# Writes of the attention outputs to DRAM issued by ScalarE instead of SyncE

## The reference, cut to what matters

```python
h = modulate(ln(x))
q, k, v = split(h @ W_qkv)            # 16 heads of 16
a = softmax(q @ k.T * 0.25 + mask)    # L0, L1, L3: all 1024 keys; L2: windows of 128
x = x + gate * ((a @ v) @ W_o)
h = modulate(ln(x))
a = softmax(q(h) @ k(ctx).T * 0.25)   # 77 keys; L2 keeps the 16 largest scores
x = x + gate * ((a @ v(ctx)) @ W_co)
x = x + gate * mlp(modulate(ln(x)))
```

## Time and profile before

| | |
|---|---|
| median of 3 runs | 3085.87 us (3081.41 to 3093.61) |
| profiled execution, device time | 3097.3 us |
| its span, first to last instruction | 3095.5 us |
| TensorE busy | 2704.0 us (87%) |
| VectorE busy | 2005.2 us (65%) |
| ScalarE busy | 1401.0 us (45%) |
| GpSimd busy | 644.9 us (21%) |
| DMA, mean busy share of 16 engines | 30% |
| mean granted TensorE clock | 0.907 |

### The profile page before, as it was taken

The page is one execution under the profiler, slowest core; times in us unless marked ns, Lnnn a source line. Parts: engine busy times, 40 slices in busy tenths (PEclk is TensorE's granted clock), DMA queues, the critical chain, the costliest instruction groups (busy, mean ns, idle before and its releaser), DMA issues.

```text
span 3095.5 us, 44651 instructions
## 1 busy us (share of the span) xinstructions
PE 2704.0 (87%) x13376; PEld 1240.5 (40%) x13376; DVE 2005.2 (65%) x4844; ACT 1401.0 (45%) x2569; POOL 644.9 (21%) x968
## 2 busy tenths in 40 slices
PE   6999999998799998989978767686679999999899
PEld 4433333335322533324454444554424342332456
DVE  6678488441668366765455568666896858886631
ACT  3255555661446464664534223322223736667341
POOL 1010011301221010131124134524312110112320
PEclk9799999899779998999988876797779999999799
DMA  6222214311532122332065424431121223122521
GB/s 211 63 63 63 79 36 135 117 31 59 176 92 62 59 78 87 103 106 65 28 187 173 112 78 149 136 93 37 64 89 32 60 51 109 53 63 88 158 84 36
DMA packets 254276, 275.90 MB, mean 89 GB/s; under 512 B 60485, under 2 KB 195423, under 8 KB 253663
## 3 DMA queue, kind: packets, MB, share of 16 engines
q1 hardware_dynamic: 242783, 271.58, 29.6%
q0 software_dynamic: 11264, 1.46, 0.3%
HBM read 157.36 MB, written 114.09 MB: 88 GB/s over the span
## 4 chain that ended last, share of the span: by engine, by line
PE 67%; DVE 16%; DMA 7%; issue 5%; POOL 2%; ACT 2%; SPq 2%; DVEq 0%; ACTq 0%; POOLq 0%
PE ring_a L1238 11%; PE ring_c L1312 10%; PE ring_b L1282 10%; PE ring_b L1335 7%; PE ring_a L1347 7%; PE ring_b L1281 4%; PE ring_a L1324 4%; PE ring_b L1196 3%; DVE row_max L1582 3%; DMA q_ring<-neg_max_parts 2%; PE ring_a L1335 1%; PE ring_b L1306 1%; DMA q_ring<-scr_q 1%; DVE bn_stats L1490 1%; PE ring_b L1270 1%
## 5 line engine op out<-in xcount | busy, mean ns | idle before, releaser
L1417 ACT ACTIVATE probs<-ring_b 128x512 f32<-128x512 f32 (+1 forms) x1728 | 906.3, 604 | 561.7 <-PE ring_b L1282 486.2
L1582 DVE TENSOR_REDUCE row_max<-ring_a 128x1 f32<-128x1024 f32 x512 | 602.8, 1219 | 133.9 <-PE ring_a L1238 130.6
L1282 PE MATMUL ring_b<-q_ring,k_ring 100*128 100x512 bf16 x1536 | 522.0, 389 | 24.0 <-DMA q_ring<-neg_max_parts 9.9
L1238 PE MATMUL ring_a<-k_ring,q_ring 96*128 96x512 bf16 x1536 | 481.7, 406 | 43.1 <-DVE row_max L1582 27.5
L1312 PE MATMUL ring_c<-probs,v_and_ones 128*17 128x512 f32 x3072 | 404.2, 605 | 3.6 <-ACT probs L1417 3.5
L1579 DVE CUSTOM_DVE_ANT_0 w_mlp<-ring_a,w_mlp 128x1024 bf16<-128x1024 f32 x256 | 302.8, 1222 | 72.9 <-PE ring_a L1238 71.0
L1693 POOL CAST neg_max_parts<-neg_max 16x128 bf16<-16x128 f32 x112 | 32.2, 287 | 1506.3 <-ACT neg_max L1411 1251.1
L1626 DVE TENSOR_TENSOR x_tok<-x_tok,ring_a 128x512 f32<-128x512 f32 x96 | 65.8, 687 | 364.1 <-PE ring_a L1347 210.3
L1238 PEld LDWEIGHTS ring_a<-k_ring,q_ring 96*128 96x128 bf16 x1536 | 129.7, 100 | 379.9 <-issue 302.8
L1282 PEld LDWEIGHTS ring_b<-q_ring,k_ring 100*128 100x128 bf16 x1536 | 146.3, 99 | 305.8 <-issue 198.0
L1335 PE MATMUL ring_b<-h_feat,w_mlp 128*128 128x512 f32 x512 | 236.3, 611 | 2.1 <-ACT h_feat L1391 1.7
(11 more groups left out here) (140 smaller groups left out, 3218.6 us busy)
## 6 DMA issues: line engine op xcount, KB each, us to landing
q_ring<-scr_q SPq DMA_DIRECT2D x128, 384.0 KB, 4.0
scr_q<-split SPq DMA_DIRECT2D x64, 384.0 KB, 3.1
k_ring<-scr_k SPq DMA_DIRECT2D x64, 384.0 KB, 4.9
scr_q<-split SPq DMA_DIRECT2D x64, 256.0 KB, 3.2
scr_out<-out_stage SPq DMA_DIRECT2D x128, 128.0 KB, 2.5
scr_out<-out_stage SPq DMA_DIRECT2D x64, 256.0 KB, 2.3
h_feat<-scr_out SPq DMA_DIRECT2D x56, 256.0 KB
reciprocals<-scr_recip SPq DMA_DIRECT2D x56, 256.0 KB
```

The source lines that it names most:

```text
L1238: last = mm(ps[:, half * BLOCK:(half + 1) * BLOCK], q[0:PARTS, h, t * P:(t + 1) * P], k_view(g)[0:PARTS, h, half * BLOCK:(half + 1) * BLOC ...
L1282: last = mm(ps[:, :], k_view(g)[0:ROWS, h, s.kt * P:(s.kt + 1) * P], q[0:ROWS, h, q0:q0 + BLOCK], start=not g.masked, stop=True)
L1417: f(PT[0:n, s.pt, :], ps[0:n, :], ACT.Exp, **kw).then_inc(b_evac, 1)
L1582: v.tensor_reduce(NM[:, s.nm, s.u:s.u + 1], ps, AX.X, ALU.max).then_inc(a_evac, 1)
```

## The change

The branch `put` moves from SP's program to ScalarE's. The list of steps, the condition and the DMAs stay as they are. On ScalarE's list a put now stands where the plan has it: after the copy into `out_stage` and often after one to three further ScalarE instructions of other steps.

```diff
         @block.sync
-                elif s.kind == "put":
-                    g, pv = s.g, s.of
-                    if "bn" in pv:
-                        sp.wait_ge(b_evac, pv.bn + 1)
-                    else:
-                        sp.wait_ge(c_evac, pv.c_n + 1)
-                    h0 = g.heads[0]
-                    n = len(g.heads) * VROWS
-                    for k, blk in enumerate(g.blks):
-                        sp.dma_start(O_SCR[g.b, h0:h0 + len(g.heads), :, blk * BLOCK:(blk + 1) * BLOCK].rearrange("h r t -> (h r) t"),
-                                     OST[k * n:(k + 1) * n, s.ost, :]).then_inc(ost_out[s.ost], 16)
         @block.scalar
+                elif s.kind == "put":
+                    g, pv = s.g, s.of
+                    if "bn" in pv:
+                        act.wait_ge(b_evac, pv.bn + 1)
+                    else:
+                        act.wait_ge(c_evac, pv.c_n + 1)
+                    h0 = g.heads[0]
+                    n = len(g.heads) * VROWS
+                    for k, blk in enumerate(g.blks):
+                        act.dma_start(O_SCR[g.b, h0:h0 + len(g.heads), :, blk * BLOCK:(blk + 1) * BLOCK].rearrange("h r t -> (h r) t"),
+                                     OST[k * n:(k + 1) * n, s.ost, :]).then_inc(ost_out[s.ost], 16)
```

## The result

The kernel after took 3114.18 us (median of 4 runs, 3108.43 to 3121.13) beside 3089.24 us of the kernel before in the same comparison (4 runs): ratio 1.0085, 95% interval 1.0054 to 1.0115, or +26 us. The change makes the kernel 0.7 to 0.9% slower. The forecast had the sign, and at +8 us too small a size, by a factor of about 3. 3114 lies in the stated range, and it is the number of the rival "full price", but that rival's mechanism is not what happened. The forecast's own band, 3083 to 3102, does not hold it: that the stated range does is owed to the room left for a rival which was wrong, and is luck.

The account below looks back on a forecast made before the run. TensorE, busy 87% of the span, was taken to bound the kernel. Terms 10 + 2 + 0 + 0 - 1 - 3 gave +8 us: 3105.3 us for the profiled execution, 3094 us carried to the median, range 3075 to 3118.

Parts of the forecast that it names:

- full price: Rival: on ScalarE the issue begins only when the exponential before it has ended; +28 us, 3114 us, chance 0.22.
- The forecast's own band: The span of the main case, a short stall of ScalarE: 3083 to 3102 around 3094 us, chance 0.48.
- SyncE gains nothing: On SP's queue, losing 192 issues (96 us) and the waits before them was counted as nothing.
- The landings give 3 us: Two put landings on the chain, 6.45 and 5.21 us, would shorten: 3 us gained, bounds 0 and 6.9.
- The last rival: Faster: SP's query loads no longer share its queue with puts, so their landings shorten; -17 us, 3069 us, chance 0.10.
- ScalarE prepares ahead, but not past an exponential that waits: On ScalarE, a put's issue can run beside an exponential that has begun, but not pass one still waiting.
- the cheap rival: Issues cost ScalarE under 0.5 us for two, or pass a waiting exponential, starting at the copy's end; 3083 us, chance 0.20.
- The forecast of 0.66 us late: At one full self-attention put, a pair's issue of 1.14 us makes ScalarE's next exponential 0.66 us late.
- The size of the loss: Full self-attention, 48 puts: TensorE loses 0.3 us on average at 33, 0 at the other 15; 10 us.
- The term for window and cross puts: Six back-to-back window puts at 0.3 us give 2 us; the 64 cross-attention puts 0, at most 2.
- the 1 us given back: A small part of TensorE's loss falls in front of a wait that exists anyway: minus 1 us.
- Later puts and what follows: Puts go out up to 1.5 us later, with `dense` and reciprocals following: 0, at most 5 us.

Follow-up runs that it names:

- e6: The kernel after, with SyncE still waiting for each copy where it issued the put but issuing nothing: +18 us over the kernel before.
- e9: The kernel after, unchanged, measured a second time: ratio 1.0066, +20 us over the kernel before.
- e10: e6 measured again, the kernel after with SyncE's old waits left in: ratio 1.0066, +20 us over the kernel before.
- e1: Against the kernel before, only the 48 full self-attention puts moved to ScalarE, window and cross-attention puts on SyncE: +21 us.
- e3: The kernel after, but ScalarE issues only the first DMA of each pair and SyncE the second: 0 us over the kernel before.
- e7: The kernel after, but each pair's second DMA issued two exponentials later or before another kind of step: +3 us over the kernel before.

## Why the prediction was right and wrong

*SyncE gains nothing: right.* e6, e9 and e10 show it from both sides.

*The landings give 3 us: not borne out.* The two landings of the earlier trace rows did get shorter, by 3.6 us together, but four are on the chain now, 14.3 us in sum where it was 11.7 (pieces of the chain after):

```profile
1357.98 4.25 DMA scr_out<-out_stage
...
1664.74 3.85 DMA scr_out<-out_stage
...
1965.92 4.26 DMA scr_out<-out_stage
...
1992.34 1.98 DMA scr_out<-out_stage
```

Over all landings nothing changed: median 2.4 and longest 7.9 us, as in the earlier trace rows. This agrees with the rule of the Trainium skill on issuing engines (DMA: Bandwidth & Descriptors, "Issuing engines are not separate DMA queues") that the prediction weighs. The last rival's premise fails with it: landings of queries of 8.07, 7.96 and 7.42 us are on the chain after, too.

*ScalarE prepares ahead, but not past an exponential that waits: right.* The issue starts with the exponential at 2747.69, not at the end of the copy at 2747.19 (the cheap rival), nor at the end of the exponential at 2748.29 (the full price). By the wait queue of the Trainium skill (Perfetto Trace Analysis, "Per-instruction lifecycle"), as the prediction reads it, the issue would have passed the waiting exponential; at this put it did not. It did pass two that had their scores and had not begun (the issue at 2694.14), which the prediction did not foresee. The forecast of 0.66 us late was measured as 0.70.

*The size of the loss: this term was mis-sized.* "TensorE has about 0.2 us of slack, so it loses about 0.45", and then "0.3 us as the mean" over 33 puts and 0 for the other 15. The slack was read at the second matmul of the three, and there it was about right (about 0.4 lost); the third had none that counts. In the earlier trace rows the three exponentials end near 2728.21, 2728.70 and 2729.18, and the third matmul, which refills the slot of the last of them, started at about 2729.35. Its weights were loaded at 2729.30, 0.12 us after the exponential's end; in the kernel after, where TensorE surely waits, the weights of the second and the third follow the ends near 2749.49 and 2749.98 by 0.12 and 0.11. So the third was already paced by ScalarE, and the delay of 0.70 went to TensorE as 0.68. The mean, too, was cut for cover that is often not there. Two puts of L3 with three exponentials in between cost nothing, but the three such puts in the first fifteen of L0 cost 0.57 to 0.58 us each: what covers an issue is exponentials that already have their scores, and a run of them without a gap does not show that. The second example of the prediction, the put at 2675.3, of which it says "It is the same", is one of the two that cost nothing (the rows from 2693.47 above). An ordinary put costs 0.6 to 0.7, one with a long issue more. That makes 0.54 a put in L3, 0.43 in the first puts of L0, and 0.43 over all 48. The term of 10 us measured 21 (e1), with an interval of 13 to 28. The term for window and cross puts, 2, measured 4 with an interval from -2 to 10. With these two the sum is 21 + 4 = 25, against 20 and 26 measured; the 3 us of the landings and the 1 us given back are below what these runs resolve.

*Later puts and what follows: small, as taken.* VectorE waited 87.0 us for reciprocals before, 89.3 after; e3 and e7 send puts as late, and lose nothing.

## What to carry to other kernels

Where an engine feeds the bound one through a short ring, what counts is not its busy share (45% here) but the longest stop that the ring covers at that point. Look for the place where the bound engine's next instruction already starts right behind the release, and take the slack there, over all slots of the ring and not the first one that one finds. Of several DMA issues on a computing engine, put work between any two: two in a row cost 20 us and more here, the same two with two exponentials between them nothing that could be measured. And when a stretch serves as a ruler, compare it piece by piece: 1.5 of the 9.1 us here were a change of clock that came without the puts too.

## What the runs showed of the hardware

A DMA issue on ScalarE took 0.32 us at the least, 0.45 us in the median and up to 1.67 us, much as on SyncE (0.32, 0.50 and 1.89 us). It did not start before an exponential that still waited for its scores, and it did start ahead of two that had them. It runs beside the compute instruction that started just before. A pair of 1.10 us held the next instruction back by 0.70 us; a single issue of 0.45 us by 0.06 us (row of the tile `out_stage` after):

```profile
L1431 ACTq DMA_DIRECT2D scr_out<-out_stage x192: 321/453/1672, 162.0 to 3023.6; - x192
```
